# Wide causal attention with its scores as three rounded products, and buffers that are shared to make room

## The chip, the cores and the metric

One core of one Trainium2 chip runs the whole program, once per run. The metric is the device time of that run in microseconds. TensorE multiplies, VectorE, ScalarE and GpSimd work on tiles, SyncE only issues transfers and keeps waits. The engines run beside each other and meet at semaphores.

## What is computed

The reference is a chain of eight stages on a residual stream of 2 x 512 tokens with 256 features: attention with a compressive memory, a mixture of experts, wide causal attention, experts, grouped attention, experts, grouped attention, experts. The change touches only the third, the wide causal attention with 16 heads of 128 features, in float32:

```python
scale = 1.0 / np.sqrt(dh).astype(np.float32)
q = (x @ Wq + bq).reshape(b, h, t, dh)
k = (x @ Wk + bk).reshape(b, t, h, dh).transpose(0, 2, 3, 1)
v = (x @ Wv + bv).reshape(b, t, h, dh).transpose(0, 2, 1, 3)
logits = jnp.einsum('bhtd,bhds->bhts', q, k) * scale
mask = jnp.triu(jnp.full((t, t), -jnp.inf, dtype=x.dtype), k=1)
weights = jax.nn.softmax(logits + mask, axis=-1)
out = jnp.einsum('bhts,bhsd->bhtd', weights, v)
out = out.transpose(0, 2, 1, 3).reshape(b, t, h * dh)
return out @ Wo + bo
```

The query keeps the order of its memory (it is reshaped, not transposed), so a head's 512 query rows come from one run of 32 tokens with all 16 blocks of features.

## The kernel before

The stage is `wide_stage`. Its heads are worked off in four groups of four (`GROUPS`, `GROUP`); within a group the two batches b follow each other as two units, and a unit is four heads. Each engine has its own program for a unit (`unit`), and these programs keep step by semaphores only.

Projections (`fill`) multiply rounded parts: `product` adds three matmuls, high part by high part, high by rest and rest by high, each in the rounded format fp32r. While a unit runs, TensorE slips the fills of the next unit between the heads' steps (`fills_of_step`, `next_fills`): in unit b = 0 of a group the keys and values of b = 1 (two fills per head), in unit b = 1 the queries of the next group for both batches, and the keys and values of its b = 0 (four fills per head: queries in heads 0 and 1, keys in head 2, values in head 3). All of these go through one bank, `fill_bank`, so each fill waits until the one before it has been read out. Keys are read out by ScalarE (`k_evacuated`), queries and values by VectorE (`evacuated`); the second batch's queries wait in `q_next`, from where GpSimd copies them to `q` (`move_q`) when the first batch's scores no longer need the place.

A head's step on TensorE (`unit` under `@block.tensor`): turn the normalised probabilities (`turn`, line 1273), multiply the next head's scores (`scores`, line 1260) between these, attend (line 1279), project the output (`project_out`). Scores are float32 matmuls in four row blocks of 128, 256, 384 and 512 columns; line 1262 adds the causal mask. VectorE finds row maxima (line 1467), ScalarE exponentiates (line 1376), VectorE normalises in place (`normalise`, line 1477, from SBUF to SBUF), ScalarE brings the turned probabilities back (line 1384). VectorE also makes the rest of the output (line 1510), on which the projection waits.

GpSimd works off one list per group, written out in order: for keys, values and output weights of the next group in turn it makes high part and rest (`split`, lines 1166 and 1169), and behind the keys' and the values' split it works on pieces of the expert weights of a later stage (`ExpertSplit.piece`): load 608 columns, make high part and rest in two halves of 304, store both, and wait for the stores before the next load. 16 pieces make the whole: four ahead of group 1, and two behind each of the two splits in groups 1 to 3. A split of the output weights of group i waits until all projections of group i-1 are done; TensorE waits for the split of the values ahead of the first value fill (`w_split[1]`) and for that of the output weights ahead of a group's first projection (`w_split[2]`). SyncE loads each group's raw weights into three places (`load`).

## Time and profile before

| | us |
|---|---|
| median of three runs | 1556.51 (1552.51 to 1558.87) |
| the profiled execution, its own time | 1555.63 |
| its span, first to last instruction | 1553.9 |
| TensorE busy | 1437.0 (92%) |
| VectorE busy | 968.4 (62%) |
| ScalarE busy | 754.9 (49%) |
| GpSimd busy | 562.0 (36%) |

The wide attention runs from about 540 to 948 us of the span. The table counts over all eight stages. Matmuls are pipelined: the duration of one includes its drain, and what one costs in a row of its kind is the distance from its start to the start of the next. A float32 matmul shows as two records. A wait that a profile lists for an engine counts only if that engine, or one that waits for it, is the one that ends the stretch.

### The profile page before, as it was taken

To read this page: it belongs to the slowest core of one execution; us is meant where nothing else is said; L and a number is where in the kernel's file an instruction comes from. 1 tells how busy PE (TensorE), PEld (TensorE's weight loads), DVE (VectorE), ACT (ScalarE), POOL (GpSimd) and SP (SyncE) were. 2 spreads that over 40 slices of the span, in tenths; PEclk is the share of its full clock that TensorE was granted. 3 is DMA by queue.
4 is the path that set the end of the run, shared out by engine and by line. 5 is a ranking of instruction groups with operands and counts; after the bars stand their busy time and mean duration, and the time that the engine had idled before them with its cause. 6 is when DMAs were issued, how large, how long until landed. Compare 5 with 4: busy or idle time off the path is not lost. (4 is left out here: it accounts for less than half of the span.)

```text
span 1553.9 us, 29211 instructions
## 1 busy us (share of the span) xinstructions
PE 1437.0 (92%) x10604; PEld 1116.8 (72%) x10630; DVE 968.4 (62%) x2214; ACT 754.9 (49%) x1878; POOL 562.0 (36%) x556
## 2 busy tenths in 40 slices
PE   6999999999899989899999999999899898999897
PEld 4778777787689777777777766896555688733586
DVE  5766667666565674756566566648675563677663
ACT  5565656656245334344343443453454353489352
POOL 2835619354136345525234200472000165110173
PEclk9999999999999999999999999999999899999998
DMA  3122231212282342303112005526000343222534
GB/s 144 59 90 69 85 103 42 90 63 90 69 330 79 112 148 103 115 17 103 40 45 99 1 1 214 201 97 227 9 2 2 131 140 129 64 63 47 188 100 139
DMA packets 57454, 149.48 MB, mean 96 GB/s; under 512 B 10225, under 2 KB 24689, under 8 KB 57201
## 3 DMA queue, kind: packets, MB, share of 16 engines
q1 hardware_dynamic: 39664, 89.58, 16.8%
q0 software_dynamic: 17664, 58.21, 11.0%
q8 instruction: 80, 1.31, 0.3%
q14 instruction: 46, 0.37, 0.1%
HBM read 104.77 MB, written 38.27 MB: 92 GB/s over the span
## 5 line engine op out<-in xcount | busy, mean ns | idle before, releaser
L145 POOL TENSOR_SCALAR ln_var<-ln_moments 128x4 f32<-128x4 f32 x16 | 4.0, 252 | 392.3 <-DVE ln_moments L130 242.4
L1376 ACT ACTIVATE s_scratch<-s_bank,s_neg_max 128x128 f32<-128x128 f32 (+3 forms) x128 | 67.2, 527 | 108.7 <-DVE s_neg_max L1467 108.5
L412 POOL DMA_INDIRECT expert_rows<-s_y,s_to_row x92 | 91.2, 991 | 57.8 <-ACT s_y L736 36.7
L1467 DVE TENSOR_REDUCE s_neg_max<-s_bank 128x1 f32<-128x128 f32 (+3 forms) x128 | 59.5, 487 | 52.5 <-PE s_bank L1262 52.2
L2811 POOL TENSOR_TENSOR s_w_hi<-s_w_raw,zero 128x1024 fp32r<-128x1024 f32 x25 | 55.5, 2221 | 100.0 <-PE s_memory L81 77.1
L1260 PE MATMUL s_bank<-s_k,s_q 128*128 128x128 f32 (+3 forms) x256 | 89.8, 446 | 0.0
L953 DVE TENSOR_TENSOR s_h_e<-s_bank,s_silu_e 128x176 f32<-128x176 f32 x92 | 31.4, 341 | 83.7 <-ACT s_silu_e L724 79.7
L79 PE MATMUL s_bank<-xn_t_hi,s_w_hi 128*128 128x512 f32 x192 | 79.7, 415 | 1.2 <-DVE xn_t_lo L212 1.2
L2476 ACT ACTIVATE s_exps<-s_bank,s_rms 128x512 f32<-128x512 f32 x128 | 76.4, 696 | 3.9 <-PE s_bank L2367 3.9
L1477 DVE TENSOR_SCALAR s_scratch<-s_scratch,s_row_sum 128x128 f32<-128x128 f32 (+3 forms) x128 | 75.4, 589 | 4.5
L405 POOL DMA_INDIRECT s_xg<-normed_rows,s_from_row x64 | 63.9, 998 | 38.5 <-DVE s_from_row L848 20.2
L1279 PE MATMUL s_bank<-s_probs_t,s_v 128*128 128x512 f32 (+3 forms) x256 | 74.7, 435 | 1.7 <-ACT s_probs_t L1384 1.7
L81 PE MATMUL s_bank<-xn_t_hi,s_w_lo 128*128 128x512 f32 x192 | 75.7, 394 | 0.0
L80 PE MATMUL s_bank<-xn_t_lo,s_w_hi 128*128 128x512 f32 x192 | 75.7, 394 | 0.0
L1384 ACT ACTIVATE s_probs_t<-s_bank 128x128 f32<-128x128 f32 (+3 forms) x128 | 48.9, 438 | 51.2 <-PE s_bank L1273 51.2
L3341 POOL TENSOR_TENSOR s_e_hi<-s_e_lo,zero 128x304 fp32r<-128x304 f32 x64 | 42.7, 685 | 85.2 <-DMA s_e_lo<-in_experts 85.2
L1279 PEld LDWEIGHTS s_bank<-s_probs_t,s_v 128*128 128x128 f32 x256 | 47.6, 190 | 30.5 <-issue 17.2
L3179 DVE SCALAR_TENSOR_TENSOR s_sigma_qt<-s_exp_part,s_positive 128x512 f32<-128x512 f32 x32 | 50.8, 1594 | 26.6 <-ACT s_positive L3090 26.5
L2030 DVE TENSOR_REDUCE s_neg_max<-s_pair 128x2 f32<-128x1024 f32 (+3 forms) x64 | 51.5, 822 | 23.4 <-PE s_pair L1804 22.6
L2814 POOL TENSOR_TENSOR s_w_lo<-s_w_raw,s_w_hi 128x1024 fp32r<-128x1024 f32 x25 | 63.5, 2539 | 2.0
L1166 POOL TENSOR_TENSOR s_w_hi<-s_w_raw,zero 128x1024 fp32r<-128x1024 f32 x11 | 20.8, 1893 | 115.1 <-PE s_bank L81 66.9
L80 PE MATMUL s_bank<-s_expert_w_lo,s_xe_hi 128*128 x184 | 59.6, 324 | 0.0
(429 smaller groups left out, 4852.5 us busy)
## 6 DMA issues: line engine op xcount, KB each, us to landing
s_expert_w_lo<-experts_lo SPq DMA_DIRECT2D x32, 608.0 KB, 13.1
s_e_lo<-in_experts POOLq DMA_DIRECT2D x32, 304.0 KB, 3.1
experts_hi<-s_e_hi POOLq DMA_DIRECT2D x32, 304.0 KB, 2.5
experts_lo<-s_e_lo POOLq DMA_DIRECT2D x32, 304.0 KB, 2.9
s_expert_w_hi<-experts_hi SPq DMA_DIRECT2D x16, 608.0 KB, 12.2
s_w_raw<-in_wa_o SPq DMA_DIRECT2D x16, 512.0 KB, 3.5
s_yg<-expert_rows SPq DMA_DIRECT2D x32, 256.0 KB, 4.5
s_raw<-in_shared SPq DMA_DIRECT2D x16, 384.0 KB, 6.4
```

Source lines behind the costliest of these rows:

```text
L79: pe.matmul(out, sh, mh, start=first, stop=False, skip_group_check=True)
L80: pe.matmul(out, sh, ml, start=False, stop=False, skip_group_check=True)
L81: return pe.matmul(out, sl, mh, start=False, stop=last, skip_group_check=True)
L405: pool.indirect_dma_start(out=rows_in(i), out_offset=None, in_=x_rows[:, :], in_offset=bass.IndirectOffsetOnAxis(ap=from_row[:, i:i + 1].b ...
L412: pool.indirect_dma_start(out=y_rows[:, :], out_offset=bass.IndirectOffsetOnAxis(ap=to_row[:, i:i + 1].bitcast(U32), axis=0), in_=y[:, i % ...
L1260: pe.matmul(to, q[:, b, h * S + r * P:h * S + (r + 1) * P], k[:, b, h, 0:(r + 1) * P], start=r == UNIT_ROWS[u][0], stop=False, skip_group_ ...
L1279: last = pe.matmul(o_bank[:, j * P:S], v[:, b, j, h * DH:(h + 1) * DH], probs_t[:, j, j * P:S], start=j == 0, stop=j == TB - 1, skip_group ...
L1376: act.activation(probs[:, h % 2, r, 0:(r + 1) * P], score_bank(h, r), ACT.Exp, bias=neg_max[:, 4 * h + r:4 * h + r + 1], accum_out=row_sum ...
L1467: dve.tensor_reduce(neg_max[:, 4 * h + r:4 * h + r + 1], score_bank(h, r), AX.X, ALU.max, negate=True).then_inc(max_done, 1)
L1477: dve.tensor_scalar(mine, mine, one, None, ALU.mult).then_inc(probs_done, 1)
L2476: act.activation(exps[:, s % 2, g, :], s_bank[g][:], ACT.Exp, scale=rms[:, b, 1, j:j + 1]).then_inc(exp_done, 1)
L2814: pool.tensor_tensor(w_lo[:, slot, :], w_raw[:, slot, :], f32(w_hi[:, slot, :]), ALU.subtract).then_inc(w_split[slot], 1)
```

## The change

Queries and keys are no longer kept in float32, but as high part and rest (`q_hi`, `q_lo`, `k_hi`, `k_lo`), and the scores are three rounded products each. The scale of the scores goes into the query weights. ScalarE rounds the keys and the first batch's queries (two instructions per query fill, `high_queries`), and VectorE makes the rests (`low_keys`, and two instructions per query fill); the second batch's queries go to `q_next` as before, and GpSimd now makes two instructions of its move, high part and rest. A fill's place is free when the rest has been made (`k_lo_done`, `q_done`).

To make room, the probabilities are packed without the unused upper blocks, `probs_t` lies in the same tile, `q_next` lies in the tile of the normalised stream, the raw weights have two places instead of three (keys and output weights share one), and a piece of expert weights has half the columns: 32 pieces of 304 columns, eight ahead of group 1 and four behind each of the two splits. VectorE's wait for the output bias moves from before the units to the first addition to the stream.

```diff
-        q_next = sb("q_next", [P, GROUP * S])
-        q, k, v = sb("q", [P, B, GROUP * S]), sb("k", [P, B, GROUP, S]), sb("v", [P, B, TB, WIDE])
+        q_next = norm.xn[:].rearrange("p t d -> p (t d)")
+        q_hi, q_lo = sb("q_hi", [P, B, GROUP * S], F32R), sb("q_lo", [P, B, GROUP * S], F32R)
+        k_hi, k_lo = sb("k_hi", [P, B, GROUP, S], F32R), sb("k_lo", [P, B, GROUP, S], F32R)
...
-            expert_split = ExpertSplit(nc, ctx, sem, name, res, t["experts1"], t["experts1_parts"], E_PART)
+            expert_split = ExpertSplit(nc, ctx, sem, name, res, t["experts1"], t["experts1_parts"], E_PART // 2)
...
-                    sp.wait_ge(w_split[p], i)
-                    sp.dma_start(w_raw[:, p, :], group_w[p][bass.ds(i, 1), :, :].rearrange("a p n -> (a p) n")).then_inc(w_loaded[p], 16)
+                    sp.wait_ge(*((w_split[1], i) if p == 1 else (w_split[0], i + 1)))
+                    sp.dma_start(w_raw[:, p % 2, :], group_w[p][bass.ds(i, 1), :, :].rearrange("a p n -> (a p) n")).then_inc(w_loaded[p], 16)
...
-                pool.tensor_tensor(q[:, 1, :], q_next[:], res.zero[:].broadcast_to([P, GROUP * S]),
+                pool.tensor_tensor(q_hi[:, 1, :], q_next, res.zero[:].broadcast_to([P, GROUP * S]),
                                    ALU.add).then_inc(q_moved, 1)
+                pool.wait_ge(q_moved, 2 * i + 1)
+                pool.tensor_tensor(q_lo[:, 1, :], q_next, f32(q_hi[:, 1, :]), ALU.subtract).then_inc(q_moved, 1)
...
-                for n in range(4):
-                    expert_split.piece(pool, n, n // 2, n % 2 * E_PART, n == 0)
+                for n in range(8):
+                    expert_split.piece(pool, n, n // 4, n % 4 * (E_PART // 2), n == 0)
             for i in range(1, GROUPS):
                 for p in range(3):
                     split(i, (p,))
                     if by_run and p < 2:
-                        for n in range(4 * i + 2 * p, 4 * i + 2 * p + 2):
-                            expert_split.piece(pool, n, n // 2, n % 2 * E_PART)
+                        for n in range(8 * i + 4 * p, 8 * i + 4 * p + 4):
+                            expert_split.piece(pool, n, n // 4, n % 4 * (E_PART // 2))
...
-                    pe.matmul(to, q[:, b, h * S + r * P:h * S + (r + 1) * P], k[:, b, h, 0:(r + 1) * P],
-                              start=r == UNIT_ROWS[u][0], stop=False, skip_group_check=True)
+                    rows, keys = slice(h * S + r * P, h * S + (r + 1) * P), slice(0, (r + 1) * P)
+                    product(pe, to, (q_hi[:, b, rows], q_lo[:, b, rows]), (k_hi[:, b, h, keys], k_lo[:, b, h, keys]),
+                            r == UNIT_ROWS[u][0], False)
...
+            def high_queries(i, f, bank):
+                act.wait_ge(q_ready, Q_FILLS * i + f + 1)
+                for j in range(2):
+                    s = 2 * f + j
+                    last = act.activation(q_hi[:, 0, :].rearrange("p (t s) -> p s t", s=HEADS)[:, s, :],
+                                          bank[:, j * B * P:j * B * P + P], ACT.Identity, bias=bq[:, s:s + 1])
+                last.then_inc(q_hi_done, 1)
...
+            def low_keys(U, b, f, bank):
+                dve.wait_ge(k_done, GROUP * U + f + 1)
+                dve.scalar_tensor_tensor(k_lo[:, b, f, :], bank[:], bk[:, f:f + 1], f32(k_hi[:, b, f, :]),
+                                         ALU.add, ALU.subtract).then_inc(k_lo_done, 1)
...
+                    dve.wait_ge(q_hi_done, Q_FILLS * i + f + 1)
+                    dve.tensor_tensor(q_next.rearrange("p (t s) -> p s t", s=HEADS)[:, subs, :], from_[:, :, 1, :],
+                                      spread(bq[:, subs], P), ALU.add)
+                    for j in range(2):
+                        mine = lambda x: x[:, 0, :].rearrange("p (t s) -> p s t", s=HEADS)[:, 2 * f + j, :]
+                        last = dve.scalar_tensor_tensor(mine(q_lo), from_[:, j, 0, :], bq[:, 2 * f + j:2 * f + j + 1],
+                                                        f32(mine(q_hi)), ALU.add, ALU.subtract)
                     last.then_inc(q_done, 1)
...
             def add_to_stream(U, b):
+                dve.wait_ge(bo_added, 1)
...
-            dve.wait_ge(bo_added, 1)
             units(dve, unit)
```

On GpSimd, from the move of the first group's queries to the end of the first piece of expert weights, before (`s_e_lo` is the raw piece and later the rest, `experts_hi` and `experts_lo` are in HBM):

```order
L1176 TENSOR_TENSOR s_q<-s_q_next,zero 128x2048
L1185 TENSOR_TENSOR x<-x,s_bo 128x2048
L3336 DMA s_e_lo<-in_experts 128x608
L3341 TENSOR_TENSOR s_e_hi<-s_e_lo,zero 128x304 x2
L3345 TENSOR_TENSOR s_e_lo<-s_e_lo,s_e_hi 128x304 x2
L3346 DMA experts_hi<-s_e_hi 128x608
L3348 DMA experts_lo<-s_e_lo 128x608
```

and now:

```order
L1185 TENSOR_TENSOR s_q_hi<-s_ln_xn,zero 128x2048
L1188 TENSOR_TENSOR s_q_lo<-s_ln_xn,s_q_hi 128x2048
L1196 TENSOR_TENSOR x<-x,s_bo 128x2048
L3375 DMA s_e_lo<-in_experts 128x304
L3380 TENSOR_TENSOR s_e_hi<-s_e_lo,zero 128x152 x2
L3384 TENSOR_TENSOR s_e_lo<-s_e_lo,s_e_hi 128x152 x2
L3385 DMA experts_hi<-s_e_hi 128x304
L3387 DMA experts_lo<-s_e_lo 128x304
```

The move has a second instruction ahead of the bias, and the last five rows, over half the columns, come eight times in place of four before the key weights of group 1 are split.

On TensorE, the first three score blocks of the first head, before:

```order
L1260 MATMUL s_bank<-s_k,s_q 128x128
L1262 MATMUL s_bank<-causal,ident_bf 128x128
L1260 MATMUL s_bank<-s_k,s_q 128x256
L1262 MATMUL s_bank<-causal,ident_bf 128x128
L1260 MATMUL s_bank<-s_k,s_q 128x384
L1262 MATMUL s_bank<-causal,ident_bf 128x128
```

and now:

```order
L79 MATMUL s_bank<-s_k_hi,s_q_hi 128x128
L80 MATMUL s_bank<-s_k_lo,s_q_hi 128x128
L81 MATMUL s_bank<-s_k_hi,s_q_lo 128x128
L1274 MATMUL s_bank<-causal,ident_bf 128x128
L79 MATMUL s_bank<-s_k_hi,s_q_hi 128x256
L80 MATMUL s_bank<-s_k_lo,s_q_hi 128x256
L81 MATMUL s_bank<-s_k_hi,s_q_lo 128x256
L1274 MATMUL s_bank<-causal,ident_bf 128x128
```

One float32 matmul per block (two records in a trace) has become three rounded ones, shown here for the first two blocks.

On VectorE, around the first query fill of head 0 in a unit b = 1, before:

```order
L1477 TENSOR_SCALAR s_scratch<-s_scratch,s_row_sum 128x384
L1449 ISA
L1453 SCALAR_TENSOR_TENSOR s_q<-s_bank,s_bq 128x2x128
L1453 SCALAR_TENSOR_TENSOR s_q_next<-s_bank,s_bq 128x2x128
L1510 TENSOR_TENSOR s_o_lo<-s_bank,s_o_hi 128x512
```

and now (`s_ln_xn` holds what `s_q_next` held):

```order
L1515 TENSOR_SCALAR s_scratch<-s_scratch,s_row_sum 128x384
L1483 ISA
L1487 TENSOR_TENSOR s_ln_xn<-s_bank,s_bq 128x2x128
L1491 SCALAR_TENSOR_TENSOR s_q_lo<-s_bank,s_bq,s_q_hi 128x128 x2
L1549 TENSOR_TENSOR s_o_lo<-s_bank,s_o_hi 128x512
```

Between the last normalisation and the rest of the output there stands one instruction more, and the first of them waits for ScalarE.

## Rows read from the trace of the kernel before

**Rows 1.** Windows, TensorE alone: stretch, length, busy (instructions), granted clock, DMA share, GB/s.

```profile
670.00:720.00 50.00, 50.00 (x257) 1.00 0.09 30
...
641.00:651.00 10.00, 6.53 (x29) 0.83 0.25 80
```

**Rows 2.** Timeline of TensorE: start us, us, engine, line, operation, operands, count.

```profile
598.52 1.02 PE L1260 MATMUL s_bank<-s_k,s_q 128*128 128x512 f32 x2
...
599.38 0.22 PE L1262 MATMUL s_bank<-causal,ident_bf 128*128 128x128 bf16 x1
...
599.73 0.39 PE L80 MATMUL s_bank<-xn_t_lo,s_w_hi 128*128 128x512 f32 x1
...
599.96 0.40 PE L81 MATMUL s_bank<-xn_t_hi,s_w_lo 128*128 128x512 f32 x1
...
1096.86 0.59 PE L1764 MATMUL s_pair<-s_ident_r,s_shift 128*128 128x128 f32 x4
```

**Rows 3.** Timeline of GpSimd in the wide attention; in brackets idle time before, and releaser.

```profile
568.42 3.60 POOL L1176 TENSOR_TENSOR s_q<-s_q_next,zero 128x2048 f32<-128x2048 f32 x1 [4.11 <-DVE s_q_next L1453]
...
574.90 4.50 POOL L1185 TENSOR_TENSOR x<-x,s_bo 128x2048 f32<-128x2048 f32 x1 [2.88 <-DMA x<-x_mid]
...
579.35 0.72 POOL L3336 DMA_DIRECT2D s_e_lo<-in_experts  x1
...
640.61 1.90 POOL L1166 TENSOR_TENSOR s_w_hi<-s_w_raw,zero 128x1024 fp32r<-128x1024 f32 x1
...
642.59 2.34 POOL L1169 TENSOR_TENSOR s_w_lo<-s_w_raw,s_w_hi 128x1024 fp32r<-128x1024 f32 x1
...
709.66 0.56 POOL L3336 DMA_DIRECT2D s_e_lo<-in_experts  x1
...
712.84 1.33 POOL L3341 TENSOR_TENSOR s_e_hi<-s_e_lo,zero 128x304 fp32r<-128x304 f32 x2 [2.62 <-DMA s_e_lo<-in_experts]
...
714.14 1.63 POOL L3345 TENSOR_TENSOR s_e_lo<-s_e_lo,s_e_hi 128x304 fp32r<-128x304 f32 x2
...
719.39 0.54 POOL L3336 DMA_DIRECT2D s_e_lo<-in_experts  x1 [2.58 <-DMA experts_lo<-s_e_lo]
```

**Rows 4.** Timeline of TensorE, groups 0 and 1: query fill, value fill, projection.

```profile
646.12 0.41 PE L79 MATMUL s_bank<-xn_t_hi,s_wq_hi 128*128 x1 [3.47 <-DVE s_q_next L1453]
...
670.53 0.48 PE L79 MATMUL s_bank<-s_w_hi,xn_t_hi 128*128 128x512 f32 x1
...
689.77 0.28 PE L79 MATMUL s_bank<-s_w_hi,s_o_hi 128*128 128x256 f32 x1
```

**Rows 5.** Timeline of VectorE: normalisation of probabilities (line 1477) at four places.

```profile
575.26 4.23 DVE L1477 TENSOR_SCALAR s_scratch<-s_scratch,s_row_sum 128x128 f32<-128x128 f32 x1
...
640.14 2.53 DVE L1477 TENSOR_SCALAR s_scratch<-s_scratch,s_row_sum 128x256 f32<-128x256 f32 x1
...
684.52 3.10 DVE L1477 TENSOR_SCALAR s_scratch<-s_scratch,s_row_sum 128x128 f32<-128x128 f32 x1
...
778.49 3.10 DVE L1477 TENSOR_SCALAR s_scratch<-s_scratch,s_row_sum 128x128 f32<-128x128 f32 x1
```

**Rows 6.** Timeline of ScalarE, VectorE and TensorE: evacuations of fills and outputs.

```profile
591.37 0.68 ACT L1371 ACTIVATE s_k<-s_bank,s_bk 128x512 f32<-128x512 f32 x1
...
599.35 0.69 DVE L1510 TENSOR_TENSOR s_o_lo<-s_bank,s_o_hi 128x512 fp32r<-128x512 f32 x1 [2.10 <-ACT s_o_hi L1410]
...
631.02 0.57 DVE L1453 SCALAR_TENSOR_TENSOR s_q_next<-s_bank,s_bq 128x256 f32<-128x256 f32 x1
...
631.65 0.39 PE L79 MATMUL s_bank<-xn_t_hi,s_wq_hi 128*128 x1 [0.19 <-DVE s_q_next L1453]
```

**Rows 7.** DMA issues by line: count, KB each, median us to landing.

```profile
s_w_raw<-in_wa_o SPq DMA_DIRECT2D x16, 512.0 KB, 3.5
...
s_q_rows<-s_q_both SPq DMA_DIRECT2D x56, 64.0 KB, 2.0
```

67 lines of the change are left out of this document (40 added, 27 removed).

## The prediction

> **What bounds the kernel now.** I read the busy time by stretch first. In the wide attention TensorE is busy for all of 670 to 720 us at full clock [rows 1], matmul behind matmul, and a group of four heads and two batches takes 94 us (one and the same instruction of two groups stands at 684.52 and 778.49 [rows 5]). So TensorE bounds this stage, and what is taken off it counts, as long as nobody else comes late. Second I read the order of time around one head for the price of a matmul. A float32 score of 512 columns is two passes, 0.86 us from its start to that of the next instruction (598.52 to 599.38 [rows 2]). A rounded product of 512 columns takes 0.23 (599.73 to 599.96), and four of 128 columns in another stage take 0.59 with the last one's drain, so 0.11 to 0.15 each [rows 2]. Third I read GpSimd in order of time, since the change gives it the most new work. It splits the weights of the next group and, between these, pieces of expert weights for a later stage. A piece of 608 columns takes 9.73 us from issue to next issue (709.66 to 719.39), 5.2 of it waits for its load (2.6) and its stores (2.6) [rows 3]. Before, GpSimd has time in hand: the value weights of group 1 are split from 640.61 on (1.90 and 2.34 us [rows 3]), done at 645, and TensorE first uses them at 670.53 [rows 4]; it projects with group 1's output weights from 689.77 [rows 4].
>
> **The change, part by part.**
>
> *Scores.* Per head 1280 columns in scores of 128, 256, 384 and 512: before 1280 x 0.86/512 = 2.15 us; after, three products each: 3 x (0.11 + 0.12 + 0.17 + 0.23) = 1.89, with 256 and 384 columns in proportion to 512. That is 0.26 less a head, 8 us over 32 heads, on TensorE and so on the path. The bounds are 0 (128 columns at 0.15, and as much more on each other form for its stationary operand) and 13 (all in proportion to 512 columns: 1.73).
>
> *Keys and queries.* Every key tile gets a second evacuation on VectorE: its nearest row is the low part of the output, 0.69, behind ScalarE's 0.68 [rows 6]. VectorE has room, but the one bank that fills go through is released later. In a head with key fills of the next group the following fill stands only behind 0.7 us of scores, while the evacuation takes 0.69 + 0.69 + 0.1: about 0.8 us lost at the third fill and 0.2 at the fourth. A query fill is now read by ScalarE (two instructions of 128 columns; 0.35 to 0.7, I take 0.5) and then by three VectorE instructions, one of 256 and two of 128 columns, where there were two of 0.57 [rows 6]; TensorE waited 0.19 for these already [rows 6], and will wait about 0.9 more per head. Two query heads and one key head in the second half of each of groups 0 to 2: 2 x 0.9 + 1.0 = 2.8 us, three times. At nothing, these evacuations would need another bank.
>
> *Start.* Before the first query VectorE now makes two more low parts (1.4 us), and ScalarE steps in: the last query lands 2.3 us later (bounds 1.4 and 3), behind 568.42. Then GpSimd moves it in two instructions instead of one: 3.60 [rows 3] and a subtraction, which for 1024 columns takes 2.34 [rows 3], so 4.6 for 2048. The addition of the output's bias (4.50) follows; its copy of the stream comes 3 to 4 us later too, since the third weight load now waits for the key split, but that is under the move. So the first piece is issued not at 579.35 [rows 3] but at 583.7. VectorE's wait for the bias moves out of the way, which gives nothing: its normalisation was blocked just as long (4.23 us, until 579.49 [rows 5]), and will be until 583.7.
>
> *Pieces of half the size, twice as many: the step that decides.* Compute: two pairs of instructions over 304 columns take 1.33 and 1.63 [rows 3], so 0.67 and 0.82 each; against 1.90 and 2.34 for 1024 columns [rows 3], 152 columns less save 0.26 and 0.32 each, in all 1.15 us a piece. The three issues (0.55 each) stay. Transfers: 64 KB land in 2.0 us, 512 KB in 3.5 [rows 7], so 152 KB less saves 0.5, for the load and for the last store: 1.0. A piece takes 9.73 - 1.15 - 1.0 = 7.6 us. The bounds are 8.6 (waits as before) and 6.0 (waits halved); the transfers' rows put it between, nearer the upper one. The notes speak against the change here: the Trainium skill, DMA: Bandwidth & Descriptors (Anatomy of one DMA), gives about 2.0 us fixed plus bytes/436e3 for a transfer that GpSimd issues, so half of 304 KB would save only 0.36; with that a piece would be an estimated 7.9 us and the sum below 4.5 us longer. Before, 304 KB land in about 3.2 us here [rows 3], somewhat above that fit's 2.7; no row shows 152 KB.
>
> GpSimd's list up to group 1's output weights has 16 pieces where it had 8, and three splits of 4.3 us. The store wait of the piece ahead of a split is hidden by it (2.1 each). Before, this reckoning gives 579.35 + 6 x 9.73 - 2 x 2.6 + 4.3 = 636.8 for the start of the value split; the row says 640.61, so I add 3 us for disturbances. After: value weights ready at 583.7 + 12 x 7.6 + 2 x 4.3 - 2 x 2.1 + 2 = 681, where TensorE, left alone, wants them at about 670 to 675 [rows 4]; output weights at 583.7 + 16 x 7.6 + 3 x 4.3 - 3 x 2.1 + 3 = 715, where it wants them at 689.77. Two stalls, of some 8 and 13 us, and up to here only GpSimd's list counts: **+25.2 us**. What TensorE saved or lost before is swallowed by it. Key weights of group 1 are ready at 648, in time.
>
> Later groups: GpSimd's splits and pieces need 3 x 4.3 + 8 x 7.6 + 8.2 - 4 = 78 us a group, the group takes 94, and the order lets it start at the same place as before; so no further stall (at 8.6 us a piece, a few us).
>
> *After the second stall.* A stall of 3.47 us before [rows 4] left the clock at 0.83 on average in 641 to 651 [rows 1], that is 1.7 us of work: **+1.7**. The subtraction added to the move meets VectorE's normalisation: its 128-column instruction waited 3.10 us (684.52) until the move ended [rows 5], without cost. With 4.6 us more on GpSimd the next normalisation waits again (one gets through between two GpSimd instructions: 640.14, done 642.67 [rows 5]), the low part of the output behind it on VectorE comes at about 693 in the place of 689, and the projection waits some 3.8 us, in groups 2 and 3: **+7.6** (bounds 0 and 14). The 22 heads left save 5.7, the fills of two groups lose 5.6: **0**.
>
> Sum: 25.2 + 1.7 + 7.6 + 0 = 34.5 on the profiled execution's own 1555.63 us (span 1553.9, under 1 us from the median 1556.51): **1590**. With 8.6 us a piece the list ends 15 us later and the sum is 1605; with 6.4 it ends 17 us earlier, 1573.
>
> **Rivals.** (a) *GpSimd just in time.* If a piece takes under 6.0 us, no weights are late; then start +4.4, scores -8, fills +8.4, moves +11.4, and the stall at 646 with its slow clock (5.2 [rows 1, 4]) may not come back: 1567, or 1555 if the moves cost nothing. For it speaks that 8.2 of a piece's 9.7 us are waits and instructions over data that halve; against it that 64 KB take 2.0 us [rows 7]. (b) *The saving arrives: faster.* The same condition (pieces under 6.0 us), and evacuations and moves hidden by the slack that VectorE shows [rows 5]: 1555.6 - 8 = 1547. It decides at the value split's end: if it is before 670, this is open. (c) *No gain in the products.* If three rounded products take as long as two float32 passes, only the last 22 heads show it: 1596, inside the range. (d) *Worse*: pieces at 8.6 with stalls in every group, over 1606.
>
> **How the numbers follow.** Forecast 0.72 (1573 to 1606, (c) with it), (a) 0.15, (b) 0.07, (d) 0.06. The range 1563 to 1606 leaves out (b), (d) and the low end of (a), near 0.16. A measurement tells about 0.5% (8 us) from no change. Faster by more is (b), 0.07; within it is the part of (a) below 1564, 0.07; slower 0.86.
>
> **What would show it.** Right: 32 pieces at 7 to 8 us; TensorE idle for some 10 us twice, about 670 to 682 and 700 to 715, the first matmul behind each with the value or output weights of group 1; the move's second instruction near 4.6 us; VectorE's 128- or 256-column normalisation at 4 us or more in three groups; score products 0.23 apart. Wrong: pieces near 6 us, GpSimd waiting for TensorE before group 1's output split, or TensorE's idle time in small parts on query fills.

## The result: 3.5% slower, and the rows behind it

The changed kernel takes 1611.79 us (median of four runs, 1605.33 to 1614.3) where the kernel before takes 1557.69; the ratio is 1.0349, with a 95% interval of 1.0315 to 1.0382. That is 54 us more. The prediction said 1590 in a range of 1563 to 1606: the direction was right, the size fell outside the range. The profiled execution takes 1614.30 us.

The page of the changed kernel, its first lines (busy time, share of the span, instructions):

```profile
span 1612.2 us, 29785 instructions
...
PE 1442.9 (90%) x10731; PEld 1137.8 (71%) x10758; DVE 1001.1 (62%) x2278; ACT 776.8 (48%) x1942; POOL 618.3 (38%) x672
```

TensorE has about as much to do as before (1437.0 us then), but a span that is 58 us longer: it waits. To see where, I use one mark in every head, the moment at which ScalarE starts on the high part of the head's output. The timeline of ScalarE, first the changed kernel, then the kernel before (start, duration, engine, line, operands, idle time before and releaser):

```profile
598.93 0.60 ACT L1432 ACTIVATE s_o_hi<-s_bank 128x512 fp32r<-128x512 f32 x1 [1.47 <-PE s_bank L1291]
...
820.28 0.60 ACT L1432 ACTIVATE s_o_hi<-s_bank 128x512 fp32r<-128x512 f32 x1 [1.37 <-PE s_bank L1291]
...
837.89 0.60 ACT L1432 ACTIVATE s_o_hi<-s_bank 128x512 fp32r<-128x512 f32 x1 [1.44 <-PE s_bank L1291]
```

```profile
588.73 0.60 ACT L1410 ACTIVATE s_o_hi<-s_bank 128x512 fp32r<-128x512 f32 x1 [1.47 <-PE s_bank L1279]
...
781.57 0.60 ACT L1410 ACTIVATE s_o_hi<-s_bank 128x512 fp32r<-128x512 f32 x1 [1.38 <-PE s_bank L1279]
...
791.56 0.60 ACT L1410 ACTIVATE s_o_hi<-s_bank 128x512 fp32r<-128x512 f32 x1 [1.47 <-PE s_bank L1279]
```

From one mark to the next is one head. The marks of all 32 heads give this table (the figures of the forecast are those of the prediction's sum):

| stretch, mark to mark | before, us | after, us | difference | forecast |
|---|---|---|---|---|
| to the first output | 588.73 | 598.93 | +10.2 | |
| group 0 | 98.87 | 110.59 | +11.7 | |
| head 0 of group 1 | 10.00 | 22.28 | +12.3 | these three: +26.9, measured +34.2 |
| rest of group 1 | 83.97 | 88.48 | +4.5 | |
| head 0 of group 2 | 9.99 | 17.61 | +7.6 | +3.8 |
| rest of group 2 | 84.11 | 88.42 | +4.3 | |
| head 0 of group 3 | 9.99 | 17.49 | +7.5 | +3.8 |
| rest of group 3 | 56.16 | 55.30 | -0.9 | the three rests: 0, measured +7.9 |
| behind the stage | 612.08 | 613.10 | +1.0 | 0 |

Now the waits themselves. The timeline of TensorE in the changed kernel, in order of time; in brackets the idle time ahead of the instruction and what ended it:

```profile
563.29 0.58 PE L79 MATMUL s_bank<-xn_t_hi,s_wq_hi 128*128 128x256 f32 x1 [3.56 <-DVE s_k_lo L1466]
...
589.61 1.53 PE L1285 MATMUL s_bank<-ident,s_scratch 128*128 128x128 f32 x5 [4.19 <-DVE s_scratch L1515]
...
690.50 0.77 PE L79 MATMUL s_bank<-s_w_hi,xn_t_hi 128*128 128x512 f32 x1 [8.61 <-POOL s_w_lo L1178]
...
722.61 0.55 PE L79 MATMUL s_bank<-s_w_hi,s_o_hi 128*128 128x256 f32 x1 [10.90 <-issue]
...
765.03 0.39 PE L79 MATMUL s_bank<-xn_t_hi,s_wq_hi 128*128 x1 [1.34 <-DVE s_q_lo L1491]
...
768.86 0.39 PE L79 MATMUL s_bank<-xn_t_hi,s_wq_hi 128*128 x1 [0.74 <-DVE s_q_lo L1491]
...
826.36 0.80 PE L79 MATMUL s_bank<-xn_t_hi,s_w_hi 128*128 128x512 f32 x1 [5.34 <-DVE s_k_lo L1466]
```

The third and fourth rows are the two stalls that the forecast puts into group 1: 8.6 us for the split value weights, 10.9 us for the output weights. The others are the first: the start (563.29 and 589.61), then 5.3 us ahead of a key fill in head 0 of group 2 (group 3 has the same with 5.27 at 932.32), and small waits on query fills.

GpSimd in the changed kernel, its timeline: the start's three long instructions and the first piece, one undisturbed piece, and the second halves of the two splits that TensorE waited for:

```profile
576.72 3.60 POOL L1185 TENSOR_TENSOR s_q_hi<-s_ln_xn,zero 128x2048 fp32r<-128x2048 f32 x1 [11.84 <-DVE s_q_lo L1491]
...
580.40 4.55 POOL L1188 TENSOR_TENSOR s_q_lo<-s_ln_xn,s_q_hi 128x2048 fp32r<-128x2048 f32 x1
...
584.91 4.49 POOL L1196 TENSOR_TENSOR x<-x,s_bo 128x2048 f32<-128x2048 f32 x1
...
589.35 0.68 POOL L3375 DMA_DIRECT2D s_e_lo<-in_experts  x1
...
622.77 0.55 POOL L3375 DMA_DIRECT2D s_e_lo<-in_experts  x1 [1.87 <-DMA experts_lo<-s_e_lo]
...
625.32 0.83 POOL L3380 TENSOR_TENSOR s_e_hi<-s_e_lo,zero 128x152 fp32r<-128x152 f32 x2 [1.99 <-DMA s_e_lo<-in_experts]
...
630.14 0.54 POOL L3375 DMA_DIRECT2D s_e_lo<-in_experts  x1 [1.87 <-DMA experts_lo<-s_e_lo]
...
688.02 2.34 POOL L1178 TENSOR_TENSOR s_w_lo<-s_w_raw,s_w_hi 128x1024 fp32r<-128x1024 f32 x1
...
720.17 2.34 POOL L1178 TENSOR_TENSOR s_w_lo<-s_w_raw,s_w_hi 128x1024 fp32r<-128x1024 f32 x1
```

A piece takes 7.37 us from issue to issue (622.77 to 630.14) against 9.73 before [rows 3]. The value weights are ready at 690.4 and the output weights at 722.5, and TensorE goes on at 690.50 and 722.61. (The bracket of the second wait names no releaser; that it is the output weights is read from these two times and from the semaphore `w_split[2]` that stands ahead of a group's first projection.) Not every piece is undisturbed: of the 16 up to the output weights, four take 8.8 to 9.5 us.

VectorE in the changed kernel: a row of the start, then the head 0 of group 2. While GpSimd moves the second batch's queries, two normalisations take 3.38 and 4.53 us, and the rest of the keys, which the fill's bank waits for, stands behind them:

```profile
556.66 4.00 DVE L1471 SCALAR_TENSOR_TENSOR s_wq_lo<-s_scratch,s_wq_hi 128x2048 fp32r<-128x2048 f32 x1 [1.05 <-ACT s_wq_hi L1371]
...
817.10 3.38 DVE L1515 TENSOR_SCALAR s_scratch<-s_scratch,s_row_sum 128x128 f32<-128x128 f32 x1
...
820.58 4.53 DVE L1515 TENSOR_SCALAR s_scratch<-s_scratch,s_row_sum 128x256 f32<-128x256 f32 x1
...
825.56 0.74 DVE L1466 SCALAR_TENSOR_TENSOR s_k_lo<-s_bank,s_bk,s_k_hi 128x512 fp32r<-128x512 f32 x1
```

In the kernel before only one normalisation met the move, and it waited 3.10 us without cost [rows 5].

Last the granted clock of TensorE, in windows (stretch, length, busy with instructions, granted clock, DMA share, GB/s), behind the start's wait, and around the wait in group 2:

```profile
563.20:568.60 5.40, 5.31 (x25) 0.50 0.18 52
820.70:826.30 5.60, 0.32 (x3) 0.85 0.00 0
826.30:831.50 5.20, 5.14 (x18) 0.50 0.00 0
831.50:837.00 5.50, 5.50 (x34) 1.00 0.00 0
```

After these waits TensorE runs at the lower of its two levels: the clock of 0.50 is 1.2 GHz, and the products of a key fill then stand 0.43 us apart instead of 0.23. So a wait of 5.3 us in a head costs 7.6.

### The profile page after: what moved, and what is told of

It is laid out like the page before. It is cut to its first block and busy times, and to the rows that moved or that the text cites. A ratio compares the mean times of both kernels' runs of the same rounds, so it can differ in the third digit from the quotient of the medians.

```text
span 1612.2 us, 29785 instructions
## 1 busy us (share of the span) xinstructions
PE 1442.9 (90%) x10731; PEld 1137.8 (71%) x10758; DVE 1001.1 (62%) x2278; ACT 776.8 (48%) x1942; POOL 618.3 (38%) x672
## 5 line engine op out<-in xcount | busy, mean ns | idle before, releaser
L2850 POOL TENSOR_TENSOR s_w_hi<-s_w_raw,zero 128x1024 fp32r<-128x1024 f32 x25 | 55.4, 2218 | 101.8 <-PE s_memory L81 78.3
L3380 POOL TENSOR_TENSOR s_e_hi<-s_e_lo,zero 128x152 fp32r<-128x152 f32 (+1 forms) x96 | 49.7, 536 | 109.4 <-DMA s_e_lo<-in_experts 109.4
L1291 PE MATMUL s_bank<-s_scratch,s_v 128*128 128x512 f32 (+3 forms) x256 | 76.2, 440 | 2.7 <-ACT s_scratch L1404 2.0
L1291 PEld LDWEIGHTS s_bank<-s_scratch,s_v 128*128 128x128 f32 x256 | 47.6, 191 | 33.9 <-issue 17.7
L1404 ACT ACTIVATE s_scratch<-s_bank 128x128 f32<-128x128 f32 (+3 forms) x128 | 49.1, 439 | 41.5 <-PE s_bank L1285 41.5
L3218 DVE SCALAR_TENSOR_TENSOR s_sigma_qt<-s_exp_part,s_positive 128x512 f32<-128x512 f32 x32 | 50.4, 1581 | 27.0 <-ACT s_positive L3129 26.9
L3375 POOL DMA_DIRECT2D s_e_lo<-in_experts x48 | 26.7, 557 | 95.2 <-DMA experts_lo<-s_e_lo 95.2
L79 PE MATMUL s_bank<-s_w_hi,s_o_hi 128*128 128x256 f32 x160 | 49.7, 311 | 11.6 <-issue 10.9
L3384 POOL TENSOR_TENSOR s_e_lo<-s_e_lo,s_e_hi 128x152 fp32r<-128x152 f32 (+1 forms) x96 | 59.6, 640 | 0.0
```

The lines of the kernel that those rows point to most:

```text
L79: pe.matmul(out, sh, mh, start=first, stop=False, skip_group_check=True)
L1291: last = pe.matmul(o_bank[:, j * P:S], v[:, b, j, h * DH:(h + 1) * DH], probs_t[:, j, j * P:S], start=j == 0, stop=j == TB - 1, skip_group ...
L3384: pool.tensor_tensor(self.lo[:, some], f32(self.lo[:, some]), f32(self.hi[:, some]), ALU.subtract).then_inc(self.lo_done, 1)
```

## The experiments

The theory after the result has four parts: half-size pieces make GpSimd late for group 1; the start is late by more than forecast; a GpSimd instruction of several us blocks VectorE's normalisation, and TensorE meets it at the key fill; and query fills are read out too slowly for the one bank. The rivals are that these costs hide one another, or that the lateness has a single other cause. Unless a run says otherwise, times are medians, ratios are to the kernel before on the same chip, and waits are from the profile.

**Half-size pieces alone**, in the kernel before:

```diff
-            expert_split = ExpertSplit(nc, ctx, sem, name, res, t["experts1"], t["experts1_parts"], E_PART)
+            expert_split = ExpertSplit(nc, ctx, sem, name, res, t["experts1"], t["experts1_parts"], E_PART // 2)
...
-                for n in range(4):
+                for n in range(8):
...
-                        for n in range(4 * i + 2 * p, 4 * i + 2 * p + 2):
+                        for n in range(8 * i + 4 * p, 8 * i + 4 * p + 4):
```

> The kernel before with one part of the change alone: 32 pieces of 304 columns in place of 16 of 608. Theory (GpSimd's list comes late because of the pieces): a piece takes 7.35 us as in the changed kernel, so the split of group 1's value weights starts 12 x 7.35 - 6 x 9.73 = 30 us later, about 670, and is done at 675, where TensorE wants it at 670.5; the output weights are done near 706, wanted near 694. Two waits of TensorE of some 4 and 12 us, with the slow clock behind them 20 us in all: about 1577 us. Rival (the later start, the two-part move and the shared raw weights make the list late, the pieces alone do not): no wait over 2 us before the first value fill and the first projection of group 1, and within 5 us of the kernel before.

Measured: 1581.57 us, ratio 1.0195 (1.0161 to 1.0228). The two rows of TensorE's timeline:

```profile
677.81 0.77 PE L79 MATMUL s_bank<-s_w_hi,xn_t_hi 128*128 128x512 f32 x1 [12.41 <-POOL s_w_lo L1169]
...
710.33 0.55 PE L79 MATMUL s_bank<-s_w_hi,s_o_hi 128*128 128x256 f32 x1 [10.41 <-issue]
```

Two stalls of 12.4 and 10.4 us, at the value fill and the first projection, with nothing else of the change in place. So the pieces alone bring about half of the loss; the rival falls. The first wait is three times the 4 us expected: GpSimd is done with the values at 677.8 and not at 675, and the query fill that waited in the kernel before [rows 4] does not wait here, so TensorE arrives about 5 us sooner (the second query head takes 13.7 us in place of 18.8).

**GpSimd's list in another order**, in the changed kernel:

```diff
-                for p in range(3):
-                    split(i, (p,))
-                    if by_run and p < 2:
-                        for n in range(8 * i + 4 * p, 8 * i + 4 * p + 4):
...
+            PIECES = ((0, 4, 11), (11, 13, 20), (20, 22, 29))
...
+                first, middle, last = PIECES[i - 1]
+                pieces(first, middle)
+                split(i, (0, 1))
+                pieces(middle, last)
+                split(i, (2,))
                 move_q(i)
+            pieces(29, 32)
```

> The changed kernel with GpSimd's list written in another order: key and value weights of the next group are split together after 4 pieces (groups 2 and 3: after 2), 7 pieces follow, then the output weights and the move; the last 3 pieces stand behind the last move. Theory: both waits of TensorE for weights of group 1 (8.6 and 10.9 us) go, and some 4 us of slow clock with them; the move of group 1, which the second wait had covered, now blocks VectorE as in groups 2 and 3 and costs 7.6. Net -16: about 1596 us. Rival (the list is only moved, and GpSimd is as late elsewhere): the output weights of some group or the end of the stage wait instead, and the time stays over 1605.

Measured: 1590.04 us, ratio 1.0235 (1.0205 to 1.0265), so 1.1 points less than the changed kernel. No wait for weights is left, and the move, no longer hidden by one, shows in group 1 as well; its head 0 takes 15.2 us. The heads 0 lose 5 to 6 us and not 7.6, and the first output stands 3.9 us earlier (595.02); the run is 6 us better than expected. The wait that is left, in group 1:

```profile
697.37 0.51 PE L79 MATMUL s_bank<-xn_t_hi,s_w_hi 128*128 128x512 f32 x1 [3.63 <-DVE s_k_lo L1470]
```

**The move in small instructions**, in the changed kernel:

```diff
-                pool.tensor_tensor(q_hi[:, 1, :], q_next, res.zero[:].broadcast_to([P, GROUP * S]),
-                                   ALU.add).then_inc(q_moved, 1)
+                for h in range(GROUP):
+                    some = slice(h * S, (h + 1) * S)
+                    pool.tensor_tensor(q_hi[:, 1, some], q_next[:, some], res.zero[:].broadcast_to([P, S]),
+                                       ALU.add).then_inc(q_moved, 1)
...
-                pool.tensor_tensor(q_lo[:, 1, :], q_next, f32(q_hi[:, 1, :]), ALU.subtract).then_inc(q_moved, 1)
+                    pool.tensor_tensor(q_lo[:, 1, some], q_next[:, some], f32(q_hi[:, 1, some]),
+                                       ALU.subtract).then_inc(q_moved, 1)
```

> The changed kernel with the move of the second batch's queries in eight instructions of 512 columns instead of two of 2048. Theory (VectorE's normalisation from SBUF to SBUF waits for the end of the one GpSimd instruction that runs, and one gets through at each end): it waits 1.2 us at most instead of 3.4 and 4.5, TensorE's wait of 5.3 us ahead of the second key fill in groups 2 and 3 shrinks to under 1, and the slow clock behind it goes: -12 us, about 1600 us; at the start, the addition of the bias (4.5 us) still blocks. Rival (GpSimd's whole work on SBUF blocks VectorE, however it is cut): the same time as the changed kernel.

Measured: 1595.91 us, ratio 1.0267 (1.0234 to 1.0301), 0.8 points less. VectorE's normalisations in head 0 of group 2:

```profile
816.48 0.81 DVE L1520 TENSOR_SCALAR s_scratch<-s_scratch,s_row_sum 128x128 f32<-128x128 f32 x1
...
817.40 0.96 DVE L1520 TENSOR_SCALAR s_scratch<-s_scratch,s_row_sum 128x256 f32<-128x256 f32 x1
...
818.47 1.00 DVE L1520 TENSOR_SCALAR s_scratch<-s_scratch,s_row_sum 128x384 f32<-128x384 f32 x1
```

They take 0.8 to 1.0 us each during the same move, TensorE does not wait ahead of the key fill, and the heads 0 of groups 2 and 3 take 9.77 us, 7.8 and 7.7 less than in the changed kernel. Here the block goes by the length of the instruction that it meets. The Trainium skill, SBUF — State Buffer (Who interferes with whom), has it so for VectorE and GpSimd instructions that contend for the shared pair of ports: the one that comes second waits for the whole instruction of the other. The 0.8 to 1.0 us of this run agree; a later run does not quite (below).

**Both together**, with the list slightly finer:

```diff
+            PIECES = ((0, 4, 6, 12), (12, 14, 16, 21), (21, 23, 25, 30))
...
                 for p in range(3):
+                    pieces(at[p], at[p + 1])
                     split(i, (p,))
                 move_q(i)
+            pieces(30, 32)
```

> The changed kernel with GpSimd's list in another order (pieces ahead of the key, value and output split: 4, 2 and 6 in group 1, 2, 2 and 5 in groups 2 and 3, two behind the last move) and the move in eight instructions. Theory (the late weights and the blocked normalisation are two separate costs): both gains add, 22 and 16 us, and the first head of group 1, which took 15.2 us with the list alone, falls to 9.8 as well; less some 4 us that the two have in common in groups 2 and 3: about 1572 us. Rival (one cost covers the other: once GpSimd is in time, VectorE or the output weights hold the same heads): over 1585.

Measured: 1571.47 us, ratio 1.0105 (1.0081 to 1.0129). The heads 0 of groups 1 to 3 take 9.75, 9.76 and 9.75 us. The two costs are separate, and they add: the list alone gave 21.8 us and the small moves alone 15.9, both together give 40.3.

**The start**, on top of the last:

```diff
+            dve.wait_ge(bq_loaded, 16)
+            dve.tensor_scalar(bq[:], bq[:], scale, None, ALU.mult).then_inc(bq_scaled, 1)
             for a in range(2):
+                if a:
+                    for f in (2, 3):
+                        low_keys(0, 0, f, ring[f])
                 dve.wait_ge(wq_hi_done, a + 1)
...
-            pool.tensor_tensor(res.x[:], res.x[:], bo[:].unsqueeze(1).broadcast_to([P, NT, D]), ALU.add).then_inc(bo_added, 1)
+            for tile in range(NT):
+                pool.tensor_tensor(res.x[:, tile, :], res.x[:, tile, :], bo[:], ALU.add).then_inc(bo_added, 1)
```

> The kernel of the run with list and moves, with the stage's start in another order: VectorE scales the query bias first and makes the third and fourth rest of the first keys before the second half of the query weights' rests, and GpSimd adds the output bias in eight instructions. Theory (the start is late because TensorE waits 3.6 us for those rests behind VectorE's blocked instructions, then runs at half the clock for 5 us, and because the addition of 4.5 us blocks the normalisation): the first output stands 6 to 9 us earlier, about 1565 us. Rival (the last query is late because of ScalarE's part in every query's read-out): under 2 us gained.

Measured: 1565.58 us, ratio 1.0057 (1.0039 to 1.0075). The first output's mark:

```profile
588.39 0.60 ACT L1442 ACTIVATE s_o_hi<-s_bank 128x512 fp32r<-128x512 f32 x1 [1.47 <-PE s_bank L1301]
```

588.39 us, where the run with list and moves has 596.43 and the kernel before 588.73. From 560 to 580 us the granted clock is 1.00. Not all of these 8.0 us are what the change had lost. TensorE's first scores come at 570.50 instead of 575.43 (569.84 in the kernel before); these 4.9 us are the start's own. The other 3.1 lie behind the first scores, where the long addition of the bias had blocked a normalisation. The kernel before has that block too: with the bias in eight instructions its own first output stands at 584.47 (below), 3.9 us ahead of this run. By the last mark of the stage 5.4 of the 8.0 us are left (949.77 against 955.20), as three heads of groups 0 and 1 now take 10.1 to 11.3 us; the median is 5.9 lower.

What is left against the kernel before is 8 to 9 us, and the marks put it into the second halves of the groups, groups 1 and 2 above all (in group 0 the kernel before has its own stall of 18.8 us [rows 4]). A head with query fills takes 15.9 us (13.9 before) and one with key fills 14.0 (12.9 before), while the heads with two fills take 9.75 (10.0 before). Four runs go after that, the first of them on the changed kernel, the others on this one.

**Queries copied out of the bank first**, in the changed kernel, with ScalarE's and VectorE's parts made from the copy:

```diff
+                    dve.tensor_tensor(q_own[:], from_[:, :, 0, :], spread(bq[:, subs], P), ALU.add).then_inc(q_copied, 1)
                     dve.tensor_tensor(q_next.rearrange("p (t s) -> p s t", s=HEADS)[:, subs, :], from_[:, :, 1, :],
-                                      spread(bq[:, subs], P), ALU.add)
+                                      spread(bq[:, subs], P), ALU.add).then_inc(q_read, 1)
+                    dve.wait_ge(q_hi_done, Q_FILLS * i + f + 1)
...
+                    dve.tensor_tensor(mine(q_lo), q_own[:], f32(mine(q_hi)), ALU.subtract).then_inc(q_done, 1)
```

> The changed kernel with a query fill read out of its bank by two VectorE instructions of 256 columns (the first batch's half into a small tile of its own, the second's to where it was); high part and rest are then made from that tile, behind the release of the bank. Theory (the serial read-out by ScalarE, 0.74 us, and then VectorE, 1.36 us, holds the one bank for fills): TensorE's waits of 0.7 and 1.3 us on query fills go back to the 0.2 to 0.4 of the kernel before, six query heads in groups 0 to 2 get 1.5 us each, and the start 1 us: -10, about 1602 us. Rival (key fills and the order on VectorE set the pace, not the bank): under 3 us gained.

Measured: 1616.6 us, ratio 1.0408 (1.0373 to 1.0442): no faster than the changed kernel, whose interval it overlaps from above. The first query head of a group falls from 15.9 to 14.4 us, as the theory wants; the second rises from 16.1 to 16.9, where the rest, now made from SBUF, takes 1.47 us in place of 0.64 beside GpSimd's value split, and the next query fill waits 1.94 us for the bank; and at the start eight fills pass VectorE one by one, so that TensorE waits ahead of the first scores:

```profile
579.11 0.33 PE L79 MATMUL s_bank<-s_k_hi,s_q_hi 128*128 128x128 f32 x1 [2.86 <-DVE s_q_lo L1492]
```

**Fills in a mixed order**, on the kernel of the start's run:

```diff
-        FILLS_OF = (Q_ALL + K_FILLS + V_FILLS, K_FILLS + V_FILLS)
+        MIXED = [next({"q": Q, "k": K, "v": V}[kind]) for kind in "qkqq" "qvqq" "qvkq" "kvkv"]
+        FILLS_OF = (MIXED, K_FILLS + V_FILLS)
```

> The kernel of the run with the start, with the sixteen fills of a unit b = 1 in another order: heads 0 to 3 take q k q q, q v q q, q v k q and k v k v, so that the fill with the shortest cover (0.9 us of scores) is a value or key fill and no longer a query fill. Theory (a query fill's read-out of 2.1 us holds the one bank, and only where it is covered by less than that does TensorE wait): the two query heads with 2.1 us of waits each fall to about 0.8, the key head loses its 0.8: 3 to 4 us a group, three times: -10, about 1555 us. Rival (VectorE's and ScalarE's added work per query fill sets the pace, wherever the fills stand): under 3 us gained.

Measured: 1566.98 us, ratio 1.0062 (1.0040 to 1.0083): no gain. The waits moved. The four heads of the second half take 15.3, 14.6, 15.3 and 13.4 us, where they took 15.9, 15.9, 14.0 and 13.1; the last query fill now stands directly ahead of the next group's scores, which wait for its rest:

```profile
768.17 0.33 PE L79 MATMUL s_bank<-s_k_hi,s_q_hi 128*128 128x128 f32 x1 [1.45 <-DVE s_q_lo L1507]
```

**A second order:**

```diff
-        MIXED = [next({"q": Q, "k": K, "v": V}[kind]) for kind in "qkqq" "qvqq" "qvkq" "kvkv"]
+        MIXED = [next({"q": Q, "k": K, "v": V}[kind]) for kind in "qkqq" "qvqq" "qvqk" "kvkv"]
```

> The kernel of the run with the mixed fills, with another order: q k q q, q v q q, q v q k, k v k v. Theory (each fill's wait is its read-out less its cover: a query fill waits 1.6 us behind scores, 1.0 behind a projection and nothing elsewhere, a key fill 1.05 behind scores, and the last query, which stood directly ahead of the next group's scores, waited 1.7; all with the 0.25 of TensorE's restart): 4.4 us of waits a group in place of 5.6, so -3.5 us against the mixed fills, about 1563 us. Rival (VectorE and ScalarE, with more to do per query fill, set the pace): within 1 us of the mixed fills.

Measured: 1565.86 us, ratio 1.0061 (1.0039 to 1.0084). Undecided. Group 2, which nothing disturbs, has its four heads in 57.6 us against 58.7 with the mixed order, near the 1.2 that the count of covers gives (5.6 less 4.4). In group 1 the second half's first head takes 17.9 us, because the split of the value weights meets a normalisation there:

```profile
735.12 2.43 DVE L1531 TENSOR_SCALAR s_scratch<-s_scratch,s_row_sum 128x512 f32<-128x512 f32 x1
```

```profile
735.36 1.91 POOL L1178 TENSOR_TENSOR s_w_hi<-s_w_raw,zero 128x1024 fp32r<-128x1024 f32 x1
...
737.35 2.44 POOL L1181 TENSOR_TENSOR s_w_lo<-s_w_raw,s_w_hi 128x1024 fp32r<-128x1024 f32 x1
```

TensorE then waits 2.07 us for the bank at 738.72, where the mixed order waited 0.73, and from 738.7 to 743.7 us the granted clock is 0.66. The order of fills decides where the read-outs meet GpSimd's splits, and this one meeting costs 2.6 us, more than the order gains in a group.

**One copy per query fill**, on the kernel of the start's run:

```diff
+                dve.tensor_tensor(q_both[:].rearrange("p s b t -> p s (b t)"), bank[:].rearrange("p (s c) -> p s c", s=2),
+                                  spread(bq[:, 2 * f:2 * f + 2], B * P), ALU.add).then_inc(q_copied, 1)
...
+                act.activation(own(q_hi[:, 0, :], f), q_both[:, :, 0, :], ACT.Copy).then_inc(q_hi_done, 1)
+                act.activation(own(q_next, f), q_both[:, :, 1, :], ACT.Copy).then_inc(q_taken, 1)
```

> The kernel of the run with the start, with a query fill of the loop read out by a single VectorE instruction of 512 columns into a small tile; ScalarE makes the high part and moves the second batch's half from there, and VectorE makes the rest one fill later. Theory (where query fills stand did not matter much because every read-out is long, ScalarE's and then VectorE's on the same bank; the bank's hold of 2.1 us is the cost): the hold falls to 0.7, the two query heads of each group fall from 15.9 to 13.1 or 13.4 us, six heads: -15, about 1551 us. Rival (the added work on ScalarE and VectorE, now more of it on ScalarE, delays the turned probabilities and so the attending product): heads stay over 15 us and the time over 1560.

Measured: 1572.62 us, ratio 1.0104 (1.0073 to 1.0134): 0.5 points above the start's run. The copy takes 0.69 us, but the bank is not free sooner: the copy now stands on VectorE behind the rest of the output, which waits for ScalarE, and behind the rest of the fill before. A fill that was written by 745.5 is copied from 746.94 on, and TensorE's waits for the bank are 1.22 and 0.64 us, where the start's run has 1.34 and 0.72. On top, ScalarE has two instructions more ahead of the turned probabilities. TensorE, then VectorE and ScalarE, in the query heads of group 1:

```profile
747.69 0.39 PE L79 MATMUL s_bank<-xn_t_hi,s_wq_hi 128*128 x1 [1.22 <-DVE s_q_both L1540]
...
755.59 0.65 PE L1299 MATMUL s_bank<-ident,s_scratch 128*128 128x128 f32 x4 [1.00 <-ACT s_scratch L1425]
```

```profile
746.94 0.69 DVE L1540 TENSOR_TENSOR s_q_both<-s_bank,s_bq 128x512 f32<-128x512 f32 x1
```

```profile
754.02 0.65 ACT L1411 ACTIVATE s_q_hi<-s_q_both 128x256 fp32r<-128x256 f32 x1 [1.49 <-DVE s_q_both L1540]
...
754.47 0.62 ACT L1412 ACTIVATE s_ln_xn<-s_q_both 128x256 f32<-128x256 f32 x1
...
754.90 0.94 ACT L1425 ACTIVATE s_scratch<-s_bank 128x128 f32<-128x128 f32 x3
```

The query heads of groups 0 to 2 take 15.6 to 18.0 us. What the rival names is seen: the turned probabilities, and TensorE with them, come 1.00 us late. But the theory has not been tested, since the hold that it blames did not become shorter. What a shorter hold would be worth stays open. The engines that read a fill out also carry the head's own chain, in order, and here the work that was to shorten the hold queued in it.

**Small splits**, on the last:

```diff
-                    pool.tensor_tensor(w_hi[:, p, :], w_raw[:, p % 2, :], res.zero[:].broadcast_to([P, DC * WIDE]),
-                                       ALU.add).then_inc(w_hi_done, 1)
+                    for c in range(4):
+                        pool.tensor_tensor(quarter(w_hi[:, p, :], c), quarter(w_raw[:, p % 2, :], c),
+                                           res.zero[:].broadcast_to([P, DC * WIDE // 4]), ALU.add).then_inc(w_hi_done, 1)
```

> The kernel of the run with one copy, with GpSimd's splits of 1024 columns in quarters of 256. Theory (every GpSimd instruction of 2 us or more that meets VectorE's work from SBUF to SBUF holds it up; 19 of these instructions are left in the loop): the odd heads of 10.1 to 11.4 us in groups 0 and 1 fall to 9.8, so -2 to -4 us against the run with one copy, about 1548 us. Rival (these single instructions are covered by TensorE's other work): within 2 us of the run with one copy.

Measured: 1578.11 us, ratio 1.0135 (1.0109 to 1.0162), worse again. Head 0 of group 1 takes 19.2 us. A normalisation of 512 columns took 7.53 us; GpSimd's rows of the same time, each four instructions of about 1.0 and 1.2 us:

```profile
691.47 7.53 DVE L1561 TENSOR_SCALAR s_scratch<-s_scratch,s_row_sum 128x512 f32<-128x512 f32 x1
```

```profile
689.81 4.03 POOL L1196 TENSOR_TENSOR s_q_hi<-s_ln_xn,zero 128x512 fp32r<-128x512 f32 x4
...
693.80 4.91 POOL L1201 TENSOR_TENSOR s_q_lo<-s_ln_xn,s_q_hi 128x512 fp32r<-128x512 f32 x4
```

So cutting is no remedy by itself: this normalisation did not get through between the instructions, as those of the small moves had. Shortly before it another, of 128 columns, took 2.52 us (684.48 to 687.00), while the four quarters of a split ran beside it (684.58 to 686.90).

**The same remedies without the change.** The kernel before, with the bias added in eight instructions, the move in four, and VectorE's wait for the bias ahead of the first addition to the stream (the one part of the change that stands by itself):

```diff
-            pool.tensor_tensor(res.x[:], res.x[:], bo[:].unsqueeze(1).broadcast_to([P, NT, D]), ALU.add).then_inc(bo_added, 1)
+            for tile in range(NT):
+                pool.tensor_tensor(res.x[:, tile, :], res.x[:, tile, :], bo[:], ALU.add).then_inc(bo_added, 1)
...
+                for h in range(GROUP):
+                    some = slice(h * S, (h + 1) * S)
+                    pool.tensor_tensor(q[:, 1, some], q_next[:, some], res.zero[:].broadcast_to([P, S]),
...
             def add_to_stream(U, b):
+                dve.wait_ge(bo_added, NT)
```

> The kernel before with only the remedies for blocked normalisations: GpSimd adds the output bias in eight instructions and moves the queries in four, and VectorE waits for the bias ahead of the first addition to the stream, as in the changed kernel. Theory (a GpSimd instruction of several us on SBUF blocks VectorE's normalisation in the kernel before as well, at the start for 4.2 us on the path): the first output stands about 3 us earlier, the later moves were covered: 1554 us where the kernel before has 1557. Rival (the block costs nothing here, since TensorE is late for another reason): within 1 us of the kernel before.

Measured: 1552.47 us, ratio 0.9979 (0.9955 to 1.0003), too little to tell from no change. In its profile the first output's mark stands 4.3 us earlier than before:

```profile
584.47 0.60 ACT L1413 ACTIVATE s_o_hi<-s_bank 128x512 fp32r<-128x512 f32 x1 [1.47 <-PE s_bank L1282]
```

And with the 16 whole pieces in another order as well:

```diff
+            PIECES = ((0, 2, 3, 6), (6, 7, 8, 11), (11, 12, 13, 16))
...
                 for p in range(3):
+                    pieces(at[p], at[p + 1])
                     split(i, (p,))
                 move_q(i)
```

> The kernel of the run before it, with GpSimd's 16 whole pieces in another order too (2, 1 and 3 ahead of the key, value and output split in group 1, 1, 1 and 3 in groups 2 and 3), which moves the value split of group 1 away from the normalisation at 640 us. Theory (that split's two instructions of 1.9 and 2.3 us block the normalisation there, a query fill waits 3.5 us for it, and the slow clock behind it takes 1.7): 3 to 5 us less, 1550 us, faster than both kernels. Rival (the split blocks another head as long): the same as the run before it.

Measured: 1549.3 us, ratio 0.9964 (0.9945 to 0.9982). This is the lowest median of the study, a third of a per cent under the kernel before, and it has no part of the rounded scores. What the order adds to the run before it is not shown: the two intervals overlap, and in the profiles the stage's last mark stands at 935.36 us, where the run before it has 934.02. The second query head of group 0, 18.8 us before [rows 4] and 15.1 in the run before it, takes 14.0; a head of 12.0 us has come in for one of 10.0, where the split of the key weights (603.14 to 607.4) now meets two normalisations, which take 2.08 and 2.38 us.

## Why the prediction was too low, step by step

**Scores: right.** Forecast 0.26 us a head; heads with two fills take 9.75 in place of 10.00. It does not hold for every head: the last three, which have no fills, gain 0.10, 0 and 0.14 us. The lower bound of the saving, 0, does not follow from its own prices: 0.04 us more on each form gives 3 x 0.79 = 2.37 us a head against 2.15, a loss of 7 us over 32 heads. The rows came nowhere near it.

**Pieces, the deciding step: right in mechanism and nearly in size.** 7.6 us a piece was forecast, 7.37 is an undisturbed one. The two stalls stand where they were put, with the weights that were named, and the run with half-size pieces alone shows that they need nothing else. With pieces of 7.37 us the list from its first issue to the output weights would take 125 us (16 x 7.37 + 3 x 4.3 - 3 x 1.9, the stores that a split hides); it takes 133.2, as some pieces are disturbed. I had allowed 3 us for that, and it is 8; pieces shorter than forecast give 3.7 of it back. A load of 152 KB lands in 2.5 us and a store in 2.1, where 304 KB took 3.1, 2.5 and 2.9:

```profile
s_e_lo<-in_experts POOLq DMA_DIRECT2D x32, 152.0 KB, 2.5
...
experts_hi<-s_e_hi POOLq DMA_DIRECT2D x32, 152.0 KB, 2.1
...
experts_lo<-s_e_lo POOLq DMA_DIRECT2D x32, 152.0 KB, 2.1
```

By the Trainium skill, DMA: Bandwidth & Descriptors (Anatomy of one DMA), half of 304 KB would save 0.36 us a transfer; these rows show 0.4 to 0.8, so the estimate of 7.9 a piece that follows from the page is too long; my 7.6 by rows is nearer to the 7.37.

**The start: mis-sized.** The first piece was forecast for 583.7 us and came at 589.35. I let the last query land 2.3 us later; it landed 8.3 us later. Two things were missed. The third and fourth keys' rests stand on VectorE behind the second half of the query weights' rests, which took 4.00 us beside GpSimd's split (2.36 before), so TensorE waited 3.56 us for a bank; and then it ran at 0.50 for 5.4 us. The forecast counted the added instructions' own durations, not where they stand in the queue. The row with these keys behind that instruction could have been read from the order of VectorE's instructions. Since both stalls of group 1 are set by GpSimd's list, its lateness passes through: 7.3 us too little in the first three stretches, of which 5.6 are the start. In the run that mends it, the first scores come 4.9 us earlier.

**The move: right in mechanism, half the size.** Its second instruction takes 4.50 to 4.57 us (4.6 forecast), and in groups 2 and 3 two normalisations wait. I let TensorE meet this at the projection, 3.8 us late. But the change itself puts an earlier meeting place: the key fill, whose bank VectorE's new instruction releases, queued behind the same normalisations. That is 5.3 us, and the slow clock behind it some 2 more, which I had charged to one stall and not to these. 15.1 measured for 7.6 in two groups; the small moves give it all back.

**Query fills: mis-sized.** I took 0.9 us per query head, and it is 2.2 (2.0 measured, with 0.25 saved in scores). The read-out lasts 2.1 us, since ScalarE's two instructions take 0.74 and not 0.5; I counted the place behind the scores (there TensorE has 0.9 us of other work between two fills, the read-out's cover) and overlooked the one behind the projection (cover 1.4). Each of the two now waits, 1.3 and 0.7 us. With the key heads, second halves lose about 6 us where 2.8 were forecast (5.1 in the marks, with what the scores save); the three rests were forecast at 0 and show +7.9.

So the sum 34.5 misses 7.3 at the start and the list, 7.5 at the moves and 7.9 at the fills, with 1.0 behind the stage: 58.2 of the 58.7 us between the two profiled executions. The three misses have one form. The added instructions were named, and their durations were nearly right; what was left out is a place where TensorE waits for a bank that one of VectorE's new rests sets free: the keys' rests at the start (3.56 us), the key fill at the move (5.34), the query fill behind the projection (0.74). Since all three went the same way, they added up, and the range was too narrow.

**The rivals.** GpSimd just in time fell, because pieces take 7.37 us and not under 6. Worse than 1606 was named for pieces at 8.6 with stalls in every group; it came true by another way, VectorE's queue. That the products give no gain fell with the heads of 9.75.

**What stays open.** Whether the rounded scores can pay in this kernel. The best version with them stands 0.6% above the kernel before (1.0057, 1.0039 to 1.0075): in it the sixteen heads with two fills gain some 0.25 us each where nothing disturbs them, and nine heads with query or key fills lose 1.1 to 2.0 against undisturbed ones, some 15 in all. That comparison favours it, since some of its remedies help without the change too: against the kernel before with those (0.9964) it is some 0.9 points behind. Four attempts at those fills gave nothing; none of them freed the bank sooner for every query fill, and a second bank is not tried.

## What to carry to other kernels

When two operands are split into high part and rest, price the read-out and not the products: here 0.25 us was saved in a head on TensorE, and 1 to 2 us were lost in each head whose fills are read out by two engines in turn. Price an added instruction by who stands behind it on its engine and who waits for that, and let a wait of TensorE carry the slow clock behind it (behind waits of 2.1 to 5.3 us it was 0.50 to 0.67 here). A buffer that is halved to make room doubles the fixed part of its owner's loop: 32 pieces at 7.4 us in place of 16 at 9.7.
